# Attention and experts on one core: row maxima turned by VectorE in blocks of 32x32, statistics over two tiles

## The reference, cut to what matters

```python
xn = layernorm(x)                              # x: 4 x 1024 x 256
Q = (xn @ Wq.T).reshape(16, b, s, 16)          # K and V likewise: 16 heads of 16
atten = softmax(einsum('hbqd,hbkd->hbqk', Q, K), axis=-1)
out = einsum('hbqk,hbkd->hbqd', atten, V).reshape(b, s, -1)
y = out + xn
attn = (y - mean(y, (1, 2))) / sqrt(var(y, (1, 2)) + 1e-5)   # over a whole batch entry
ffn = sum over the best two of 8 experts e of gate_e * ((xn @ w_in[e].T) @ w_out[e].T)
result = x + attn + ffn
```

## Time and profile before

| | |
|---|---|
| median of 3 runs | 1003.16 us (1002.3 to 1003.21) |
| the profiled execution's own time | 1001.28 us |
| its span, first to last instruction | 999.5 us |
| TensorE busy | 974.0 us, 97% of the span |
| VectorE busy | 780.2 us, 78% |
| ScalarE busy | 694.2 us, 69% |
| GpSimd busy | 285.1 us, 29% |
| attention stage alone, 600 to 700 us | PE 99.99, DVE 94.99, ACT 90.06, POOL 25.13 us |
| granted clock of TensorE | 1.00 in that stretch, 0.994 over the span |

### The profile page before, as it was taken

One profiled execution on the slowest core, in us unless ns is written; L12 is line 12 of the kernel. 1 busy time (PEld: TensorE's weight loads), 2 busy tenths in 40 slices (PEclk: granted clock), 3 DMA queues, 4 the chain that ended last, 5 costly groups with the idle time before them and its releaser, 6 DMA issues.

```text
span 999.5 us, 20786 instructions
## 1 busy us (share of the span) xinstructions
PE 974.0 (97%) x7816; PEld 504.5 (50%) x7816; DVE 780.2 (78%) x961; ACT 694.2 (69%) x1385; POOL 285.1 (29%) x389
## 2 busy tenths in 40 slices
PE   7999999999998999999999999999999999999994
PEld 6888888888876433333333333333333333333332
DVE  4344454543466899999999999999999999999975
ACT  2312333333322789999989899898989999899994
POOL 2001445544455222223222322223222322223222
PEclk9999999999999999999999999999999999999997
DMA  9967442223200133333333333333333333332204
GB/s 355 366 248 217 144 139 76 72 78 107 88 23 1 43 98 92 97 92 95 92 93 95 88 100 87 97 92 93 94 91 99 86 98 92 95 93 73 73 23 162
DMA packets 127043, 108.59 MB, mean 109 GB/s; under 512 B 81120, under 2 KB 102368, under 8 KB 126944
## 3 DMA queue, kind: packets, MB, share of 16 engines
q1 hardware_dynamic: 122720, 102.81, 35.4%
q10 hardware_dynamic: 4224, 4.46, 1.3%
HBM read 80.75 MB, written 42.21 MB: 123 GB/s over the span
## 4 chain that ended last, share of the span: by engine, by line
PE 96%; POOL 1%; DMA 1%; DVE 1%; issue 1%; ACT 0%; DVEq 0%; SPq 0%; ACTq 0%; POOLq 0%
PE ps L1081 28%; PE ps L1061 22%; PE ps L1007 18%; PE ps L1039 11%; PE ps L960 6%; PE ps L932 4%; PE ps L948 2%; PE ps L1097 1%; PE ps L1109 1%; PE ps L921 1%; DMA wp<-w_out_t 0%; DMA qf<-ot 0%; POOL rden L425 0%; ACT stage L534 0%; DVE xn L885 0%
## 5 line engine op out<-in xcount | busy, mean ns | idle before, releaser
L750 DVE TENSOR_REDUCE negm<-ps 128x1 f32<-128x1024 f32 x512 | 614.8, 1222 | 31.7 <-PE ps L1039 27.3
L585 ACT ACTIVATE wp<-ps 128x512 f32<-128x512 f32 x680 | 368.9, 595 | 43.7 <-PE ps L1061 6.7
L1061 PE MATMUL ps<-qf,kf 50*128 50x512 f32 x1024 | 373.1, 446 | 0.1
L1039 PE MATMUL ps<-kf,qf 48*128 48x512 f32 x1024 | 366.1, 444 | 1.0 <-DVE negm L750 1.0
L1061 PEld LDWEIGHTS ps<-qf,kf 50*128 50x128 f32 x1024 | 152.6, 185 | 199.0 <-ACT wp L585 97.5
L1081 PE MATMUL ps<-wp,vb 128*17 128x256 f32 x2720 | 212.6, 385 | 0.1
L1039 PEld LDWEIGHTS ps<-kf,qf 48*128 48x128 f32 x1024 | 147.2, 185 | 4.3 <-issue 3.9
L425 POOL TENSOR_TENSOR rden<-choice,minus 128x16 f32<-128x16 f32 x31 | 90.3, 2914 | 151.5 <-ACT choice L604 151.5
L585 ACT ACTIVATE picks<-ps 128x512 f32<-128x512 f32 x172 | 102.7, 597 | 22.8 <-PE ps L1061 5.0
L741 DVE SCALAR_TENSOR_TENSOR acc<-ps,gates,acc 128x256 f32<-128x256 f32 x64 | 30.8, 482 | 101.3 <-PE ps L1007 97.2
L1081 PEld LDWEIGHTS ps<-wp,vb 128*17 128x17 f32 x2720 | 46.0, 95 | 122.7 <-ACT vstage L585 53.2
(11 more groups left out here) (124 smaller groups left out, 898.9 us busy)
## 6 DMA issues: line engine op xcount, KB each, us to landing
qk_d<-stage SPq DMA_DIRECT2D x64, 256.0 KB
feat_d<-qk_d SPq DMA_DIRECT2D x64, 256.0 KB, 3.3
qf<-feat_d SPq DMA_DIRECT2D x128, 128.0 KB
qf<-feat_d SPq DMA_DIRECT2D x128, 64.0 KB
kf<-feat_d SPq DMA_DIRECT2D x128, 64.0 KB
v_d<-vstage ACTq DMA_DIRECT2D x8, 544.0 KB, 4.8
vb<-v_d SPq DMA_DIRECT2D x128, 34.0 KB, 2.4
acc<-x SPq DMA_DIRECT2D x8, 512.0 KB, 7.2
```

The lines of the kernel that those rows point to most:

```text
L585: nc.scalar.activation(weight_tile(n, j, b)[:, h * HALF:(h + 1) * HALF], ps[:, score_bank(score_turn[unit, b]), :], ACT.Exp).then_inc(exp_ ...
L750: nc.vector.tensor_reduce(negm[:, n % 2, qt:qt + 1], ps[:, b:b + 2, :].rearrange("p b c -> p (b c)"), AX.X, ALU.max, negate=True).then_inc ...
L1039: last = nc.tensor.matmul(ps[:, MAX_BANK[turn % 2] + half, :], qf[rows, u, qt * P:(qt + 1) * P], kf[rows, u, :], start=True, stop=True)
L1061: nc.tensor.matmul(ps[:, score_bank(score_turn[unit, half]), :], kf[rows, u, j * P:(j + 1) * P], qf[rows, u, h * HALF:(h + 1) * HALF], sta ...
```

## The change

The maxima are no longer transposed by TensorE. `mpart` becomes a tile of 128 x 32 for each of two batches, of which the halves fill the first 16 columns and zeros the rest, and VectorE transposes it in blocks of 32x32 into `mrows`. Each of the four blocks then has, on its first 16 partitions, the 32 positions of its 32 partitions. SyncE therefore brings a batch's rows together in four DMAs (the strips, a 32-position strip of every block each), into partitions 48 and 49 of `qf` alone; the rows of the other half are written by a fifth DMA (the copy), which reads `qf` and waits until the four have landed. The scores wait for all five: ROWS_IN is 16 * 5. The PSUM bank of the weighted sums no longer holds the transposed maxima, so ScalarE's `pv_out` takes 256 columns and waits neither for TensorE's transposition nor for the rows.

The second part: for the first three batch entries, `statistics` handles two tiles of 256 in one instruction of 512, every second time that it is called, and `aggregate` combines half as many results.

```diff
 def max_rows(n):                                         # SyncE
     slot = n % SLOTS
-    if n < 2:
-        sp.wait_ge(turn_done, first_turn[n] + 1)
-    else:
-        sp.wait_ge(pv_evac, n - 1)
-    for half in range(2):
-        first = half * ROWS + FR
-        sp.dma_start(qf[first:first + 2, slot, :].bitcast(FP32), ot[0:2 * NKT, 4:6, n if n < 2 else (n - 2) % HELD, :]
-                     ).then_inc(mrow_in[slot], 16)
+    sp.wait_ge(mrows_done, n + 1)
+    rows = qf[FR:SR, slot, :].bitcast(FP32).rearrange("w (q a i) -> w q a i", q=NKT, i=SQUARE)
+    for a in range(P // SQUARE):
+        sp.dma_start(rows[:, :, a, :], mrows[a * SQUARE:a * SQUARE + 2 * NKT, n % 2, :]).then_inc(mrow_in[slot], 16)
+
+def max_rows_again(n):
+    slot = n % SLOTS
+    sp.wait_ge(mrow_in[slot], ROWS_IN * (n // SLOTS + 1) - 16)
+    sp.dma_start(qf[ROWS + FR:ROWS + SR, slot, :].bitcast(FP32), qf[FR:SR, slot, :].bitcast(FP32)).then_inc(mrow_in[slot], 16)
...
 for n in range(NB - 1):
     max_rows(n + 1)
...
     if n + AHEAD < NB:
         regroup(n + AHEAD)
+    max_rows_again(n + 1)
     if n + SLOTS < NB:
...
 def max_halves(n):                                       # GpSimd
...
+    if n < 2:
+        pool.wait_ge(mpart_const, 1)
+    else:
+        pool.wait_ge(mrows_done, n - 1)
...
 def pv_out(n):                                           # ScalarE
     act.wait_ge(pv_done, NKT * (n + 1))
-    groups = 4
-    if n + 2 < NB:
-        act.wait_ge(mt_ready, n + 1)
-        act.wait_ge(mrow_in[n % SLOTS], 32 * (n // SLOTS + 1))
-        groups = 6
...
+def maxima_to_rows(n):                                   # VectorE
+    dve.wait_ge(msplit, 2 * (n + 1))
+    if n >= 2:
+        dve.wait_ge(mrow_in[(n - 2) % SLOTS], ROWS_IN * ((n - 2) // SLOTS + 1) - 16)
+    nc.vector.transpose(mrows[:, n % 2, :], mpart[:, n % 2, :].bitcast(FP32)).then_inc(mrows_done, 1)
...
 def statistics(pair):
     dve.wait_ge(y_done, pair + 1)
-    nc.vector.bn_stats(ystat[:, pair, :], xn[:, pair, :]).then_inc(ystat_done, 1)
+    if pair >= EARLY * TPB:
+        nc.vector.bn_stats(ystat[:, pair, :], xn[:, pair, :]).then_inc(ystat_done, 1)
+    elif pair % 2:
+        nc.vector.bn_stats(ystat[:, pair // 2, :], xn[:, pair - 1:pair + 1, :].rearrange("p t d -> p (t d)")).then_inc(ystat_done, 1)
...
-                    if n == 0 and qt == 2:
-                        first_rows(1)
+                    if qt == (2 if n == 0 else 1):       # in VectorE's loop of maxima
+                        maxima_to_rows(n + 1)
...
     if j == 0 and h == 0:                                # TensorE's scores
-        pe.wait_ge(mrow_in[u], 32 * (n // SLOTS + 1))
+        pe.wait_ge(mrow_in[u], ROWS_IN * (n // SLOTS + 1))
...
-def maxima_to_rows(n):                                   # TensorE, and its calls
...
```

More of the change, by code:

```diff
@@ L46, in attention_and_experts @@
     HELD = 4
+    ROWS_IN = 16 * 5
+    SQUARE = 32
     SETS = 3
@@ L120, in attention_and_experts @@
         negm = sb("negm", [P, 2, NKT])
-        mpart = sb("mpart", [P, 2, 2, NKT], FP32R)
-        ot = sb("ot", [P, 6, HELD, TB])
+        mpart = sb("mpart", [P, 2, SQUARE], FP32R)
+        mrows = sb("mrows", [P, 2, SQUARE])
+        ot = sb("ot", [P, 4, HELD, TB])
         rden = sb("rden", [P, 4, 4])
@@ L191, in attention_and_experts @@
         msplit = sem("msplit")
-        mt_ready = sem("mt_ready")
+        mrows_done = sem("mrows_done")
+        mpart_const = sem("mpart_const")
         mrow_in = sem("mrow_in", SLOTS)
@@ L208, in attention_and_experts, with max_turn @@
         o_out = sem("o_out", 4)
[L210 to L222, removed]
-                if n == 0 and qt == 2:
-                    first_turn[1] = next_turn()
-        last_turn = next_turn()
+        last_turn = NKT * NB
+        def max_turn(n, qt):
+            return NKT * n + qt
         score_turn, row_turn, turn_user = {}, {}, []
@@ L354, in _ @@
             max_rows(0)
+            max_rows_again(0)
             for n in range(NB - 1):
@@ L628, in _ @@
             nc.vector.memset(ot[:], 0.0).then_inc(att_const, 1)
+            nc.vector.memset(mpart[:].bitcast(FP32), 0.0).then_inc(mpart_const, 1)
             def token_statistics(c):
@@ L744, in maxima @@
             def maxima(n, qt):
-                turn = max_turn[n, qt]
+                turn = max_turn(n, qt)
                 if qt == 0 and n >= 2:
@@ L839, in _ @@
                         dve.wait_ge(ff_scaled[-1], 2 * NT)
-                        nc.vector.memset(ps[:, PV_BANK, 0:POS // 4 + P], 0.0).then_inc(att_const, 1)
-                    if n == 0 and qt == 2:
-                        first_rows(1)
+                        nc.vector.memset(ps[:, PV_BANK, 0:POS // 4], 0.0).then_inc(att_const, 1)
+                    if qt == (2 if n == 0 else 1):
+                        maxima_to_rows(n + 1)
                     if n % 2 == 1 and n > 1:
@@ L845, in _ @@
                             statistics((n - 3) // 2)
+            maxima_to_rows(NB - 1)
             def aggregate(part, entries):
-                dve.wait_ge(ystat_done, TPB * entries.stop)
+                dve.wait_ge(ystat_done, TPB * entries.stop - EARLY * TPB // 2)
                 for b in range(entries.start, entries.stop):
-                    last_aggr = nc.vector.bn_aggr(bmv[:, b, :], ystat[:, b * TPB:(b + 1) * TPB, :].rearrange("p t s -> p (t s)"))
+                    kept = slice(b * TPB // 2, (b + 1) * TPB // 2) if b < EARLY else slice(b * TPB, (b + 1) * TPB)
+                    last_aggr = nc.vector.bn_aggr(bmv[:, b, :], ystat[:, kept, :].rearrange("p t s -> p (t s)"))
                 last_aggr.then_inc(fin_d, 1)
@@ L1032, in max_scores @@
             def max_scores(n, qt, halves=(0, 1)):
-                u, turn = n % SLOTS, max_turn[n, qt]
+                u, turn = n % SLOTS, max_turn(n, qt)
                 if qt == 0:
@@ L1131, in _ @@
                             max_scores(n, qt)
-                            if n == 1 and qt == 1:
-                                maxima_to_rows(0)
             for n in range(NB):
@@ L1139, in _ @@
                             y_bank(NT - 1, 2 * j + h)
-                        if n == 0 and j == 1 and h == 0:
-                            maxima_to_rows(1)
                         if n == NB - 2 and j in (1, 2) and h == 0:
@@ L1147, in _ @@
                             sum_values(n - 1, NKT // 2 + j - LAG, h)
-                        if n and j == LAG - 1 and h == 1:
-                            if n + 1 < NB:
-                                maxima_to_rows(n + 1)
-                            if n % 2 == 1 and n > 1:
-                                to_token_rows((n - 3) // 2)
+                        if j == LAG - 1 and h == 1 and n % 2 == 1 and n > 1:
+                            to_token_rows((n - 3) // 2)
             for j in range(NKT // 2 - LAG, NKT // 2):
```

29 lines of the change are left out of this document (6 added, 23 removed).

## The result

The changed kernel takes 1124.28 us, the median of 4 runs (1111.81 to 1145.72), measured beside 1002.73 us of the kernel before; the ratio is 1.1105, 95% interval [1.1073, 1.1137]. Runs counted as slow (here 1133.42 and 1145.72, granted clock 0.914 and 0.901) stand in the medians of this document but not in its ratios; the median of the two others is 1113.48. The profiled execution took 1115.14 us, 1113.3 of it the span. The prediction was 1042, between 1014 and 1061: slower, as forecast, but by 114 us of span instead of 41, and well above the range.

What follows compares the result with a forecast made beforehand. TensorE bounded the kernel, VectorE close behind; two DMA hops would stretch the batch: 60 x (10.95 - 10.22) = +43.8 us, less 2.4 early and 0.5 last, +40.9 on 1001.3, so 1042, range 1014 to 1061.

Steps and rivals of the forecast that it cites:

- Mechanism of the wait: At each batch's first scores TensorE waits 0.7 to 1.2 us for a DMA into qf; period 10.8 to 11.1 us.
- Strips at 9.8 us after the loads' start: In SyncE's DMA queue the strips land behind the loads, 9.8 us after these began, between 9.3 and 10.25.
- The copy, 2.2 + 0.1 us: Second hop within qf: 2.2 us from the start of its issue to landing, 0.1 us for two wake-ups.
- 9.56 us from the scores to the loads: Time from a batch's scores to the loads they release: 9.83 us before, 9.56 without TensorE's transposition.
- Path two, 11.0 to 11.1 us: SyncE's order: the copy queues behind the regrouping DMA, issued 7.7 us into the batch and landing 3.3 us later.
- path one: Through the DMA queue: strips land behind the loads, then the copy; two batches take 21.66 us, one 10.83.
- TensorE's transposition, 0.27 us on the path: Removing 62 transpositions from TensorE in the attention loop saves 0.27 us each, 16.7 us, all on the path.
- The early part, 2.4 us back: Two early transpositions leave TensorE: 0.28 us each and a 1.85 us wait for GpSimd's halves, 2.4 us gained.
- the last two batches, 0.5: Batches 62 and 63 have no loads before them and keep their saving of 2 x 0.27 = 0.5 us.
- VectorE's transposition, 0.3 us and hidden: 64 new transpositions of 128x32 cost VectorE 0.3 us each, at most 0.42, with nothing on the path.
- The rows come in time: Rival: strips land without queueing behind the loads, the batch takes 9.95 us, 19.1 us are kept: 982; chance 0.06.
- SyncE is the whole bound: Rival: copy always behind the whole regrouping, strip issues 0.77 us, 11.5 us a batch: 1075; slower than 1061 had 0.06.

Runs made afterwards that it cites:

- fill_2: The changed kernel with two extra TensorE multiplications of no use before the wait for the rows in each of batches 2 to 61: 1057.96 us, ratio 1.0541.
- plain_regroup_turn_early: The changed kernel with plain loads of 48 rows, the regrouping issued ahead of the strips and VectorE's transposition one unit earlier: 1000.20 us, ratio 0.9948.
- after_plain_loads: The changed kernel with q and k loaded by four plain DMAs of 48 rows a batch, without broadcast loads: 1096.88 us, ratio 1.0885.
- before: The kernel before the change, unaltered: 1002.73 us beside the changed kernel, 1004.0 to 1004.2 us beside the experiments.
- copy_first: The changed kernel with the regrouping DMA issued behind the copy instead of ahead of it: 1155.0 us, ratio 1.1516.
- fill_1: The changed kernel with one extra TensorE multiplication of no use before the wait for the rows in each of batches 2 to 61: 1064.61 us, ratio 1.0590.
- no_copy: The changed kernel without the copy from batch 4 on, scores waiting for the four strips alone: 1003.84 us, ratio 1.0007.
- after: The changed kernel as it stands, against the kernel before: 1124.28 us, ratio 1.1105.

## Why the prediction was half right

- **Mechanism of the wait, and direction: right.** The chain has the DMAs into qf that the prediction named, 11% and 6% against 0%; SyncE's copy waits for the strips; the two-engine stretch is as it was. Of its other signs, TensorE's wait of 0.7 to 1.2 us in each batch came as 31 waits of up to 2.6 us in 49 batches, and the period of 10.8 to 11.1 us as (1077.7 - 350.2) / 60 = 12.13.
- **The step that failed: the clock.** My sum took every unit of TensorE at the durations of a clock of 1.00 and had no term for what waiting does to it. The rivals and the range were built from waits alone. The runs show 136 us of the loop at 0.50, and with two multiplications a batch of filler the clock is back at 1.00 and 57 of 111 us are gone (ratios 1.1105 and 1.0541). Without the clock's part the time would have been some 1058 us (`fill_2`), inside the range. Nothing in the trace of before could give the size of this term: it has single waits, of 1.85 us for one, around which the clock is at 1.00, but nowhere a loop that waits 1 us again and again. That should have widened the range upwards.
- **Strips at 9.8 us after the loads' start: low.** In the kernel before the maxima do land at 9.83 (median of 53 batches), as read. But the strips land at 10.18 (median of 56 batches, 9.58 to 10.66): the loads end at 9.43, and the last of four queued strips comes 0.7 us behind them.
- **The copy, 2.2 + 0.1 us: right.** 1.9 us and 0.06 us for the two wake-ups, but more than 2.2 and up to 2.8 us in the 22 of 56 batches in which it is issued within 1.1 us of the regrouping.
- **9.56 us from the scores to the loads: low.** Where TensorE doesn't wait (`plain_regroup_turn_early`) it is 9.47 us in even and 9.91 in odd batches, 9.69 in the mean; where it waits (`fill_2`) about 9.9. With 9.9, 10.15 and 2.0 us two batches take 22.05 us, one 11.03; with the copies that are close behind the regrouping (2.08 us in the mean) the 11.17 of `fill_2` is explained. I had 10.83 by this sum and took 10.95.
- **Path two, 11.0 to 11.1 us: right in the number, in part by luck.** It is 11.24 us (median) in `after_plain_loads`, whose regrouping moves half as many pieces more but is issued 7.3 us into the batch, not 7.7. It is not additive to path one, and in the changed kernel it seldom decides.
- **TensorE's transposition, 0.27 us on the path: mis-sized.** It was read as a step between two units; taking it away gives 0.11 us. From scores to scores (means of 25 batches each, `before` and `plain_regroup_turn_early`), the unit that held it shortens from 1.43 to 1.22 us in even batches, where the third and fifth units grow by 0.05 and 0.03, and only from 1.87 to 1.80 in odd ones, which also transpose the weighted sums there. What takes up the rest isn't settled.
- **The early part, 2.4 us back, and the last two batches, 0.5: not seen.** Batch 2 starts at 350.2 instead of 350.0 us, and from the start of batch 62 to the end both kernels take 35.6 us.
- **VectorE's transposition, 0.3 us and hidden: right**, 0.20 us. **The statistics, nothing: right.**
- **The rivals.** "The rows come in time" was the wrong case for this kernel, and its 982 too good even where they do come in time (1000.20 and 996.93). "SyncE is the whole bound" named 1075, nearer to the result, but not for its reason: with path two taken away (`copy_first`) the time didn't fall.

## What to carry to other kernels

Before a step goes into two dependent DMAs, look at what else the queue holds at that moment: here the first hop stood behind two loads on two engines and the second behind a regrouping, and both could be mended by the form of the loads and the order of issue. When a forecast leaves TensorE waiting a microsecond or more again and again in a loop that had no wait, widen the range for the clock, and test it with a multiplication of no use in front of the wait: here the clock was half of the loss. The worth of an instruction taken off a busy engine can be less than its duration: here 0.11 of 0.27 us.

## What the runs showed of the hardware

- Waits of at most 3.0 us (TensorE's weight load, 35 in 600 us of the changed kernel) went with a clock of 0.50 (1.2 GHz) for 136 us of the loop, and without them it stayed at 1.00. A single 128x128 multiplication in front of each wait, 0.28 to 0.38 us, brought back 1.00 in the loop of the traced run of `fill_1`; the same one in the middle of the batch only 0.95.
- The profiled execution of `no_copy` had a granted clock of 0.95 from its 11th to its 997th us, neither of the two levels, and yet took only 1009.46 us, beside 1001.44 to 1006.79 in the others. It is the only such trace here.
- A DMA of 8 KB from qf to qf lands 1.9 to 2.0 us after its issue started when the regrouping of 1024 pieces ahead of it was issued 1.3 us earlier or more, 2.4 to 2.8 us when 0.6 us earlier (`after`), and 3.05 us in the median right behind a regrouping of 1536 pieces (`after_plain_loads`).
